# Layer 1 attention: keys and queries turned by 32x32 blocks and memory instead of on TensorE

## The reference

```python
def _L1_attn_ref(hidden_states, Wq, bq, Wk, bk, Wv, bv, Wo, bo, gq, gk):
    B, N, D = (2, 256, 512)
    H, HD = (32, 128)
    EPS = 1e-06
    ...
    q = (hidden_states @ Wq + bq).reshape(b, n, H, HD)
    ...
    q = rmsnorm(q, gq)      # w * x * rsqrt(mean(x * x) + EPS), over HD
    k = rmsnorm(k, gk)
    scale = 1.0 / np.sqrt(HD)
    scores = jnp.einsum('bhnd,bmhd->bhnm', q, k) * scale
    attn = jax.nn.softmax(scores.astype(jnp.float32), axis=-1).astype(q.dtype)
    out = jnp.einsum('bhnm,bmhd->bnhd', attn, v).reshape(b, n, H * HD)
    return out @ Wo + bo
```

## Time and profile before

| | us |
|---|---|
| median of 3 runs | 3002.14 |
| lowest and highest | 3000.78, 3002.54 |
| the profiled execution | 3004.29 |
| its span, first to last instruction | 3002.2 |
| layer 1's attention in it, first transposes to last output tile | 1147 to 2739 |

### The profile page before, as it was taken

The page is one execution under the profiler, slowest core; times in us unless marked ns, Lnnn a source line. Parts: engine busy times, 40 slices in busy tenths (PEclk is TensorE's granted clock), DMA queues, the critical chain, the costliest instruction groups (busy, mean ns, idle before and its releaser), DMA issues. The chain is left out here.

```text
span 3002.2 us, 55475 instructions
## 1 busy us (share of the span) xinstructions
PE 2888.2 (96%) x15712; PEld 2508.9 (84%) x15712; DVE 2235.4 (74%) x3420; ACT 1593.7 (53%) x3145; POOL 1952.2 (65%) x1525
## 2 busy tenths in 40 slices
PE   7999999999999978999999999999999999987998
PEld 5888888888888757888998988999898989876886
DVE  6787887887887856777777777777777777776555
ACT  4444444444444423666666666666666666663221
POOL 7777777777777632666666666666666566655664
PEclk9999999999999999999999999999999999998999
DMA  4334334334334401666666666565666666566551
GB/s 123 116 107 120 104 107 119 105 107 119 104 107 119 126 25 51 196 200 199 202 196 204 205 195 204 195 204 195 204 200 199 208 194 204 190 196 199 151 145 41
DMA packets 310073, 464.10 MB, mean 155 GB/s; under 512 B 30464, under 2 KB 220928, under 8 KB 305792
## 3 DMA queue, kind: packets, MB, share of 16 engines
q1 hardware_dynamic: 272336, 328.37, 37.9%
q10 hardware_dynamic: 37680, 135.02, 11.4%
HBM read 293.41 MB, written 169.87 MB: 154 GB/s over the span
## 5 line engine op out<-in xcount | busy, mean ns | idle before, releaser
L1660 ACT ACTIVATE b_prob<-b_s_ps,b_shift 128x1024 f32<-128x1024 f32 x256 | 286.4, 1119 | 344.8 <-DVE b_shift L1810 337.4
L82 PE MATMUL b_pj_kq<-b_w_hi,xT_hi 128*128 128x384 f32 x1008 | 352.1, 349 | 26.7 <-DVE b_nat L1786 25.1
L83 PE MATMUL b_pj_kq<-b_w_lo,xT_hi 128*128 128x384 f32 x1008 | 343.0, 340 | 0.0
L84 PE MATMUL b_pj_kq<-b_w_hi,xT_lo 128*128 128x384 f32 x1008 | 342.6, 340 | 0.0
L1816 DVE STREAM_TRANSPOSE b_blocks<-b_prob 128x1024 f32<-128x1024 f32 x256 | 317.4, 1240 | 29.3 <-ACT b_prob L1660 28.7
L1567 POOL TENSOR_TENSOR b_rstd<-b_mean_sq,power 128x4 f32<-128x4 f32 x128 | 128.9, 1007 | 321.6 <-DVE b_mean_sq L1796 315.0
L1582 POOL TENSOR_TENSOR b_pT_lo<-b_pT_lo,b_pT_hi 128x1024 fp32r<-128x1024 f32 x128 | 305.0, 2404 | 19.6 <-ACT b_pT_hi L1649 19.1
L1582 POOL TENSOR_TENSOR pT_lo<-pT_lo,pT_hi 128x1024 fp32r<-128x1024 f32 x128 | 305.0, 2405 | 13.2 <-ACT pT_hi L1649 13.2
L1810 DVE TENSOR_REDUCE b_shift<-b_s_ps 128x1 f32<-128x1024 f32 x256 | 307.3, 1201 | 3.0 <-PE b_s_ps L84 3.0
L82 PEld LDWEIGHTS b_pj_kq<-b_w_hi,xT_hi 128*128 128x128 f32 x1008 | 190.4, 189 | 64.5 <-DVE b_nat L1786 49.5
L1341 POOL TENSOR_TENSOR b_w_lo<-b_w_raw,b_w_hi 128x512 fp32r<-128x512 f32 x96 | 124.0, 1293 | 151.9 <-ACT b_w_hi L1334 134.5
(11 more groups left out here) (345 smaller groups left out, 9389.1 us busy)
## 6 DMA issues: line engine op xcount, KB each, us to landing
bounce<-b_blocks ACTq DMA_DIRECT2D x256, 512.0 KB, 3.5
pT_lo<-bounce SPq DMA_DIRECT2D x512, 128.0 KB, 3.1
b_pT_lo<-bounce SPq DMA_DIRECT2D x512, 128.0 KB, 2.8
kv_bounce<-a_kv_blocks SPq DMA_DIRECT2D x128, 256.0 KB, 3.8
a_kv_raw<-kv_bounce SPq DMA_DIRECT2D x32, 1024.0 KB, 4.8
b_w_raw<-in_w SPq DMA_DIRECT2D x32, 768.0 KB, 5.2
b_w_raw<-in_w SPq DMA_DIRECT2D x95, 256.0 KB, 3.2
a_w_raw<-in_w SPq DMA_DIRECT2D x32, 256.0 KB, 3.1
```

The costliest lines, as they stand in the source:

```text
L82: pe.matmul(out, w_hi, x_hi, start=first, stop=False, skip_group_check=partial)
L83: pe.matmul(out, w_hi, x_lo, start=False, stop=False, skip_group_check=partial)
L84: return pe.matmul(out, w_lo, x_hi, start=False, stop=last, skip_group_check=partial)
L1660: act.activation(prob[t % 2][:, :], s_ps[t % 2][:, :], ACT.Exp, bias=shift[:, t:t + 1], accum_out=row_sum[:, t:t + 1]).then_inc(exp_done, 1)
```

## The change

- TensorE's `transpose_kq` goes. Instead VectorE turns keys and queries by 32x32 blocks (`turn_kq`, two transposes of 128x256 a batch), ScalarE's queue writes the 256 KB to memory (`write_kq`), and SP reads them back with four transfers of 64 KB (`move_kq`), a step pair later than the scaling.
- ScalarE's `kq_high` reads from SBUF and has one more operation: it scales the queries by the gain in place, then copies keys and queries. The low parts move from VectorE to GpSimd (`kq_low`).
- The operation that made means of the sums goes: `sq` has one more column that holds HD x epsilon, so the sum is HD times the mean with epsilon. The factor HD that keys and queries then lack together goes into the gain (HD^0.5 in place of HD^-0.5).
- The half bank that held the transposed keys and queries becomes a second output bank (`y_odd`); TensorE waits for the add before the last one.
- Orders and schedules: projection runs two steps earlier (`projected`), preparation one pair earlier (`prepared`), with a second buffer for the first batch (`nat_first`); VectorE takes the blocks' transposes first, then the sum, then the take; ScalarE scales behind the exponential; GpSimd puts the power between the halves of the probabilities' low part; weight slices are split in steps 0, 1, 2; SP's list of moves begins at tile 4 of the head before and has the new moves woven in.

The diff, without hunks that only rename or pass arguments on:

```diff
-        nat = [sb(f"nat{i}", [P, BATCH, KQV]) for i in range(NB)]
-        sq = sb("sq", [P, BATCH, 2, HD])
+        nat_first = [sb(f"nat0{b}", [P, BATCH, KQV]) for b in range(2)]
+        nat_rest = [sb(f"nat{i}", [P, BATCH, KQV]) for i in range(1, NB)]
+        kq_blocks = [sb(f"kq_blocks{i}", [P, GROUPS, 2, BATCH, BLK]) for i in range(2)]
+        kq_bounce = [nc.dram_tensor(f"kq_bounce{i}", (GROUPS, BLK, GROUPS, 2 * BATCH * BLK), F32) for i in range(2)]
+        kq_raw = [sb(f"kq_raw{i}", [P, GROUPS, 2, BATCH, BLK]) for i in range(2)]
+        sq = sb("sq", [P, BATCH, 2, HD + 1])
         sq_sum = sb("sq_sum", [P, BATCH, 2])
-        mean_sq = sb("mean_sq", [P, BATCH, 2])
...
-        pj_kq = bank("pj_kq", [P, TOK])
-        pj, kq_ps = pj_kq[:, 0:HALF], pj_kq[:, HALF:].rearrange("p (k n) -> p k n", k=2)
+        pj_y = bank("pj_y", [P, TOK])
+        pj, y_odd = pj_y[:, 0:HALF], pj_y[:, HALF:]
...
-            return pj if peeled(h, HEADS - 1) and t >= 3 and t % 2 else y_ps[:, :]
+            return y_odd if t % 2 else y_ps[:, :]
...
-            if s < 6:
-                return (h + 1, 1 - b, s + 2) if nxt else None
-            return (h + 2, b, s - 6) if more else None
+            if s < 4:
+                return (h + 1, 1 - b, s + 4) if nxt else None
+            return (h + 2, b, s - 4) if more else None
+        def prepared(h, b, nxt, more, s):
+            i = s // 2 + 1
+            if i < NB:
+                return (h + 1, 1 - b, i) if nxt else None
+            return (h + 2, b, 0) if more else None
+        def turned(h, b, nxt, s):
+            return (h + 1, 1 - b, s // 2) if nxt and s % 2 == 0 else None
         def quarter(h, b, cur, rest, s):
...
+        def v_batches(h, b, cur, nxt, s):
+            if s == 1:
+                return ((h, b, 3),) if cur else ()
+            which = {5: (0, 1), 7: (2,)}.get(s, ())
+            return [(h + 1, 1 - b, i) for i in which] if nxt else ()
+        SPLITS = {0: 0, 1: 1, 2: 2}
...
+            def move_kq(g, i):
+                sp.wait_ge(kq_written, 16 * (NB * g + i + 1))
+                sp.sem_inc(room, 1)
+                wait(sp, kq_lo_done, NB * g + i - 1)
+                for c in range(GROUPS):
+                    sp.dma_start(kq_raw[i % 2][c * BLK:(c + 1) * BLK].rearrange("y r k u x -> y r (k u x)"),
+                                 kq_bounce[i % 2][:, :, c, :].rearrange("r y n -> y r n")).then_inc(kq_moved, 16)
...
-                if rest:
-                    move(h - 1, NT - 1)
-                for t in range(NT - 1):
+                for t in range(NT // 2, NT):
+                    if t == 5 and cur:
+                        move_kq(h, 3)
+                    if t == 7 and nxt:
+                        move_kq(h + 1, 0)
+                    if rest:
+                        move(h - 1, t)
+                for t in range(NT // 2):
+                    if t % 2 and nxt:
+                        move_kq(h + 1, t // 2 + 1)
                     if cur:
                         move(h, t)
                     if nxt and t == 2:
...
-                pool.wait_ge(mean_ready, NB * g + i + 1)
-                wait(pool, exp_done, NT * (g - 1))
+                pool.wait_ge(means_done, NB * g + i + 1)
+                wait(pool, kq_scaled, NB * (g - 2) + i + 1)
...
+            def kq_low(g, bg, i):
+                cut = slice(i * WIDE, (i + 1) * WIDE)
+                pool.wait_ge(kq_hi_done, 2 * (NB * g + i + 1))
+                pool.tensor_tensor(in_blocks(k_lo[bg][:, cut]), from_blocks(i, 0), f(in_blocks(k_hi[bg][:, cut])),
+                                   ALU.subtract)
+                pool.tensor_tensor(in_blocks(q_lo[bg][:, cut]), from_blocks(i, 1), f(in_blocks(q_hi[bg][:, cut])),
+                                   ALU.subtract).then_inc(kq_lo_done, 1)
...
-                    if nxt and s % 2 == 0:
-                        inverse_rms(h + 1, 1 - b, s // 2)
-                    if v_batch(h, b, cur, nxt, s):
-                        v_low(*v_batch(h, b, cur, nxt, s))
+                    for which in v_batches(h, b, cur, nxt, s):
+                        v_low(*which)
+                    if nxt and s % 2:
+                        kq_low(h + 1, 1 - b, s // 2)
                     if split_batch(h, cur, rest, s):
-                        for part in range(2):
-                            prob_lo(*split_batch(h, cur, rest, s), part)
+                        prob_lo(*split_batch(h, cur, rest, s), 0)
+                    if s % 2 == 0 and prepared(h, b, nxt, more, s):
+                        inverse_rms(*prepared(h, b, nxt, more, s))
+                    if split_batch(h, cur, rest, s):
+                        prob_lo(*split_batch(h, cur, rest, s), 1)
...
-                act.wait_ge(kq_tr, NB * g + i + 1)
+                act.wait_ge(kq_moved, 16 * GROUPS * (NB * g + i + 1))
                 wait(act, scored, NT * (g - 1))
-                act.activation(k_hi[bg][:, cut], kq_ps[:, 0, :], ACT.Copy)
-                act.activation(q_hi[bg][:, cut], kq_ps[:, 1, :], ACT.Copy, scale=gain[:, 0:1]).then_inc(kq_hi_done, 1)
+                scaled = kq_raw[i % 2][:, :, 1, :, :].rearrange("p r u x -> p r (u x)")
+                act.activation(scaled, scaled, ACT.Copy, scale=gain[:, 0:1]).then_inc(kq_hi_done, 1)
+                act.activation(in_blocks(k_hi[bg][:, cut]), from_blocks(i, 0), ACT.Copy)
+                act.wait_ge(kq_hi_done, 2 * (NB * g + i) + 1)
+                act.activation(in_blocks(q_hi[bg][:, cut]), from_blocks(i, 1), ACT.Copy).then_inc(kq_hi_done, 1)
+            def write_kq(g, i):
+                act.wait_ge(kq_blocked, 2 * (NB * g + i + 1))
+                wait(act, kq_written, 16 * (NB * g + i))
+                wait(act, kq_moved, 16 * GROUPS * (NB * g + i - 1))
+                act.dma_start(kq_bounce[i % 2][:, :, :, :].rearrange("r y c n -> (r y) (c n)"),
+                              kq_blocks[i % 2][:, :, :, :, :].rearrange("p c k u x -> p (c k u x)")).then_inc(
+                    kq_written, 16)
...
                 for s in range(NT):
-                    if nxt and s % 2 == 0:
-                        square(h + 1, s // 2)
-                    if v_batch(h, b, cur, nxt, s):
-                        v_high(*v_batch(h, b, cur, nxt, s))
+                    ready = prepared(h, b, nxt, more, s)
+                    if turned(h, b, nxt, s):
+                        write_kq(h + 1, s // 2)
+                    if s % 2 == 0 and ready:
+                        square(*ready)
+                    for which in v_batches(h, b, cur, nxt, s):
+                        v_high(*which)
                     q = quarter(h, b, cur, rest, s)
                     if q and q[3]:
                         out_hi(q[0], q[2])
                     if split_batch(h, cur, rest, s):
                         for part in range(2):
                             prob_hi(*split_batch(h, cur, rest, s), part)
-                    if nxt and s % 2 == 0:
-                        scale_kq(h + 1, 1 - b, s // 2)
...
+                    if s % 2 == 0 and ready:
+                        scale_kq(*ready)
...
-            def transpose_kq(g, i):
-                pe.wait_ge(kq_scaled, NB * g + i + 1)
-                wait(pe, kq_lo_done, NB * g + i)
-                for kind in range(2):
-                    for u in range(BATCH):
-                        last = pe.transpose(kq_ps[:, kind, u * P:(u + 1) * P], nat[i][:, u, kind * HD:(kind + 1) * HD],
-                                            sh.ident[:, :])
-                last.then_inc(kq_tr, 1)
...
-                wait(pe, y_added, NT * h + (t - 1 if peeled(h, HEADS - 1) and t >= 3 else t))
+                wait(pe, y_added, NT * h + t - 1)
...
-                    if nxt and s % 2:
-                        transpose_kq(h + 1, s // 2)
...
-                dve.tensor_reduce(sq_sum[:, :, :], sq[:, :, :, :], AX_X, ALU.add).then_inc(summed, 1)
-                dve.wait_ge(summed, NB * g + i + 1)
                 wait(dve, rstd_ready, NB * g + i)
-                dve.tensor_scalar(mean_sq[:, :, :], sq_sum[:, :, :], 1.0 / HD, L1_EPS, ALU.mult,
-                                  ALU.add).then_inc(mean_ready, 1)
-            def kq_low(g, bg, i):
-                cut = slice(i * WIDE, (i + 1) * WIDE)
-                dve.wait_ge(kq_hi_done, NB * g + i + 1)
-                dve.tensor_tensor(k_lo[bg][:, cut], kq_ps[:, 0, :], f(k_hi[bg][:, cut]), ALU.subtract)
-                dve.scalar_tensor_tensor(out=q_lo[bg][:, cut], in0=kq_ps[:, 1, :], scalar=gain[:, 0:1],
-                                         in1=f(q_hi[bg][:, cut]), op0=ALU.mult,
-                                         op1=ALU.subtract).then_inc(kq_lo_done, 1)
+                dve.tensor_reduce(sq_sum[:, :, :], sq[:, :, :, :], AX_X, ALU.add).then_inc(means_done, 1)
+            def turn_kq(g, bg, i):
+                dve.wait_ge(kq_scaled, NB * g + i + 1)
+                wait(dve, kq_written, 16 * (NB * g + i - 1))
```

(37 more changed lines are left out.)

51 lines of the change are left out of this document (26 added, 25 removed).

## The result

The changed kernel takes 2919.98 us (median of four, 2919.07 to 2923.68) against 3001.46 us beside it (2999.64 to 3002.54): ratio 0.9726, 95% interval 0.9714 to 0.9738. The profiled execution took 2923.68 us, its span is 2921.6, 80.6 less than before's. The forecast was 72 us less and 2930; measured are 81.5 us less.

A forecast was written before the change was run, and what follows sets the result against it. Two close bounds: VectorE and ScalarE's hand-over loop (48.1 us a head) and TensorE (47.0). Floor 45.2 plus 0.3 of holes saves 2.6 on each of 30 heads, -78; start and head 0 +6; together -72, giving 2930, range 2914 to 2982.

The forecast's parts named there:

- TensorE's floor: TensorE's work per pair of steps: without four transposes 11.75 falls by 0.45 to 11.30 us, 45.2 a head.
- Which bound: Kernel before: TensorE sets about half the pairs (11.75 us), the hand-over between VectorE and ScalarE the others (12.31).
- the loop: VectorE and ScalarE waiting for each other in turn: 48.1 us a head before, 9.8 us a pair after.
- The means: On VectorE, the mean-square operation goes, taken as a tiny one of 0.15 to 0.2 us.
- Low parts to GpSimd: GpSimd gains two 128x256 subtractions a batch, 0.74 us taken; busy goes from 7.7 to 9.2 us a pair.
- Holes left: Time per head that TensorE still loses beyond its own work: 0.3 us taken, between 0 and 1.14.
- VectorE: VectorE gains two block transposes at 0.43 us, loses both long waits; busy goes from 9.1 to 8.9 us a pair.
- its cover: VectorE's take of a projected tile ends near 6.3 us, TensorE wants the bank at 7.7: 1.4 us hide it.
- The hop: Keys' and queries' round through memory: 10.4 us a pair, bounds 9.0 and 13.8, 0.9 us under TensorE's floor.
- Start: Before the first scores, four round trips that nothing overlaps: +11.7 us; head 0 gives -5, net +6.
- Two banks: TensorE's output tile no longer waits for the previous add; no long wait was seen there, so nothing counted.
- the hop that paces: Rival: denser DMAs lengthen landings by 1.3 us, so the memory round takes 46.8 us a head; 2968 us, chance 0.17.

The follow-up runs named there:

- the dummy transposes: Changed kernel with one output bank and four 128x128 transposes of a constant, read by nobody, put back on TensorE each odd step: 2968.18 us, ratio 0.9884.
- the lighter kernel: Changed kernel without the projection's pass over the weights' low part: 2874.27 us; also without the round through memory, 2795.13 us.

## Why the prediction held, step by step

- **TensorE's floor.** Right. 0.45 a pair from two rows; 0.43 by the dummy transposes. 45.2 a head forecast, 45.12 measured.
- **Which bound.** Wrong in part. I let TensorE set half of the pairs from one stretch between projections without a hole (11.75). Without the means the short pairs fell to 11.34, so the loop set all of them; both bounds happened to be within 0.1 there. The forecast didn't depend on it, because both are lifted; but the expected gain of taking the means away did, 12 us instead of 31.
- **The means.** Mis-sized: 0.37 to 0.42 instead of 0.15 to 0.2. I read the duration (0.17), not the spacing of starts. And a condition was missing altogether: in the new GpSimd order this operation would have been held 2 us each time. That the change takes it away is what makes its orders possible: on the kernel before, the orders alone are +150 us, the missing means alone -31, both together -27.
- **Low parts to GpSimd.** The busy time was right (742 ns against 0.74; GpSimd 80% of the stretch, 1119.0 of 1397). But I costed it as neutral, and it is worth 40 us.
- **Holes left.** I took 0.3 a head between 0 and 1.14, it is 0.18. With the floor this makes 2.84 a head where I had 2.6: 7 of the 10 us that I was off, and head 30 gave 4.2 rather than 2.6.
- **VectorE.** Block transposes 0.42 (0.43 taken). The take keeps its cover: TensorE's waits for `nat` fell from 35.1 to 1.2 us in 1000.
- **The hop.** It stayed hidden, as forecast, but not in the way that I had it. My terms add up to 10.3, not 10.4, and I took them as a loop that sets the length of each pair. TensorE asks for the blocks once a head, and the lighter kernel loses its time there. Of the terms, the 256 KB land in 2.0 us (3.6 taken), but the 64 KB reads in 3.2 (2.8 taken); the DMA share is 0.86, between 0.80 by bytes and 0.93 by packets. The round accounts for 0.15 of the 0.18 in holes, by the kernel without it. As to the latency of 2 us at high load in the Trainium skill ("DMA: Bandwidth & Descriptors", section "Latency and other measured facts"), the median landings of the probabilities' transfers grew by 0.2 to 0.6 us between share 0.62 and 0.86, far less than that. Those of the weights and biases, loaded once a head, grew by 1.7 to 2.0 (768 KB: from 5.2 to 7.1); whether that is latency or the transfers queued ahead of them no run here tells.
- **Start.** +11.7 forecast, +11.8 measured. Head 0: -5 and -4.0. That the size came out so near is luck: I had counted four idle round trips, of which 6.6 us came back when the round was taken away. The rows show TensorE's wait of 7.13 us for a weight slice, and its lower clock afterwards, neither of which was in the sum; how the 11.8 divides among them isn't tested.
- **Two banks.** Nothing, as said.

Of the rivals, the hop that paces came nearest: ScalarE's gain copy waits in 40 of 89 pairs, by the lighter kernel the margin is 1.2 us a head, and one place in SP's order is enough to lose 55 us.

## What to carry to other kernels

A wait costs what is queued behind it. Blocks up to 4 us late cost 0.15 us a head with GpSimd waiting for them, and 1.2 with VectorE; a wait of 4.9 us a pair in the queue that also loads the probabilities costs 1.7. So cost a moved operation by the queue, not by its busy time, and look where its result is first needed: here lateness counts once a head and not in each pair. And price a small dependent operation by the spacing of starts, then look whether another engine's long instruction can overlap it in the new order: a duration far above what the shape needs, ending with the other engine's, is the mark of it.

## What the runs showed of the hardware that I had not expected

- A tensor_scalar of 128x4 on VectorE takes 0.17 us alone and 1.9 to 2.4 us when GpSimd's subtraction of 128x1024 has begun, a scalar_tensor_tensor of 128x4 then takes 1.9 to 2.3; block transposes and reciprocals are not held.
- An operation of 0.17 us between two others costs about 0.4 us of the engine's time where it waits for the one ahead.
- TensorE, after 7.1 us without work at the start, runs its next two tiles of projection at a granted clock of 0.50; a tile takes 4.2 and 4.0 us instead of 2.3. What it costs the kernel isn't measured.
- With the DMA share up from 0.62 to 0.86, writes of 512 KB land in 3.8 us instead of 3.6 and reads of 128 KB in 3.4 instead of 2.8 and 3.1 (medians).
